# The logic attention's scores one step sooner, its values ahead of the last gates, and the norm and the choices of later stages regrouped

## What is computed

```python
h = concatenate([tok_ref(x), txt], axis=1)                 # 32 x 113 x 128
h = h + L0_attn_ref(layernorm(h))     # logic attention
h = h + L0_ffn_ref(layernorm(h))      # expert choice: each expert takes its best 28 rows
h = h + L1_attn_ref(layernorm(h))     # attention with relative positions
h = h + L1_ffn_ref(layernorm(h))      # 8 LSTM experts, 2 chosen for each row
```

```python
S1, S2 = q1 @ k1.T * scale, q2 @ k2.T * scale
A1, A2 = softmax(S1), softmax(S2)
Cr, Cl = log(A1 @ A2 + 1e-6), log(A2 @ A1 + 1e-6)
feat  = stack([S1, S2, S1.T, S2.T, Cr, Cl])
hid   = gelu(conv1_w @ feat + conv1_b)          # 6 -> 16, for each pair of rows and head
gates = sigmoid(conv2_w @ hid + conv2_b)        # 16 -> 4: and, or, not, chain
Smix  = S1 + g_and*S2 + g_or*(logaddexp(S1, S2) - S1) - g_not*0.5*S2 + g_chain*Cr
y     = softmax(Smix) @ v1 + w * (A1 @ (A2 @ v2))
out   = y @ proj_w
```

## Time and profile before

| | us |
|---|---|
| runs of the kernel before | median 2381.17 (2380.01 to 2381.9, 3 runs) |
| profiled execution | 2382.08 |
| its span | 2380.3 |
| front (tokens, norm) | 0 to 72 |
| logic attention | 72 to 1196 |
| norm and expert choice | 1196 to 1427 |
| relative attention | 1427 to 1641 |
| norm and LSTM experts | 1641 to 2380 |
| mean granted clock of TensorE | 0.932 |

### The profile page before, as it was taken

The page is one execution under the profiler, slowest core; times in us unless marked ns, Lnnn a source line. Parts: engine busy times, 40 slices in busy tenths (PEclk is TensorE's granted clock), DMA queues, the critical chain, the costliest instruction groups (busy, mean ns, idle before and its releaser), DMA issues. The chain is left out here.

```text
span 2380.3 us, 55433 instructions
## 1 busy us (share of the span) xinstructions
PE 2126.8 (89%) x22214; PEld 1520.6 (64%) x22214; DVE 1712.8 (72%) x2729; ACT 1664.8 (70%) x3075; POOL 334.2 (14%) x198
## 2 busy tenths in 40 slices
PE   6699999999999999998549799987789999999998
PEld 3554444544444444443137588846689999999997
DVE  4457888888888888886554344535898888888887
ACT  3478888888888888888523336732667777777776
POOL 0122222222222222221000013410000000000000
PEclk9589999999999999999759869997799999999998
DMA  6288888888888888888110000001212222122220
GB/s 181 69 246 225 235 230 221 227 227 228 234 227 220 230 225 233 230 228 202 45 45 1 10 2 2 2 24 72 83 61 69 75 75 70 65 72 70 75 75 21
DMA packets 113273, 305.20 MB, mean 128 GB/s; under 512 B 20559, under 2 KB 57545, under 8 KB 112506
## 3 DMA queue, kind: packets, MB, share of 16 engines
q1 hardware_dynamic: 113018, 301.66, 45.0%
HBM read 168.64 MB, written 80.65 MB: 105 GB/s over the span
## 5 line engine op out<-in xcount | busy, mean ns | idle before, releaser
L746 ACT ACTIVATE la_hid<-ps,la_b 128x904 f32<-128x904 f32 (+1 forms) x480 | 451.0, 991 | 105.1 <-PE ps L598 104.4
L1749 PE MATMUL ps<-ls_xm,ls_w_in_parts 128*128 128x226 f16 x3072 | 471.7, 263 | 10.5 <-DVE ls_xm L1867 5.2
L1757 PE MATMUL ps<-ls_state_parts,ls_w_rec_parts 128*128 128x226 f16 x2976 | 450.3, 260 | 0.0
L1794 ACT ACTIVATE ls_gates<-ps,ls_bias 128x226 f32<-128x226 f32 x768 | 299.3, 444 | 62.4 <-PE ps L1757 61.9
L1749 PEld LDWEIGHTS ps<-ls_xm,ls_w_in_parts 128*128 128x128 f16 x3072 | 296.6, 98 | 21.6 <-DVE ls_xm L1867 5.6
L598 PE MATMUL ps<-la_pairs,la_w 32*64 32x452 f32 x3584 | 294.0, 569 | 12.1 <-ACT la_hid L746 12.0
L1757 PEld LDWEIGHTS ps<-ls_state_parts,ls_w_rec_parts 128*128 128x128 f16 x2976 | 286.3, 96 | 7.1
L611 PE MATMUL ps<-la_hid,la_w 128*32 128x452 f32 x1856 | 242.3, 559 | 15.2 <-ACT la_opened L752 15.2
L566 POOL TENSOR_TENSOR la_P<-la_P,la_inv 113x904 f32<-113x904 f32 x64 | 107.6, 1703 | 573.8 <-DVE la_soft L896 560.6
L611 PEld LDWEIGHTS ps<-la_hid,la_w 128*32 128x32 f32 x1856 | 42.1, 108 | 195.6 <-issue 95.6
L752 ACT ACTIVATE la_opened<-ps,la_b 128x904 f32<-128x904 f32 x128 | 129.8, 1014 | 43.8 <-PE ps L611 37.5
(11 more groups left out here) (293 smaller groups left out, 4072.4 us busy)
## 6 DMA issues: line engine op xcount, KB each, us to landing
la_pairs<-la_maps SPq DMA_DIRECT2D x224, 452.0 KB, 6.5
la_gate<-la_opened SPq DMA_DIRECT2D x448, 113.0 KB, 3.5
ls_w_all<-ls_weights SPq DMA_DIRECT2D x32, 904.0 KB, 4.1
la_maps<-la_ST SPq DMA_DIRECT2D x32, 791.0 KB
la_maps<-la_S SPq DMA_DIRECT2D x32, 791.0 KB
ls_m_all<-ls_masks SPq DMA_DIRECT2D x31, 456.0 KB, 3.7
la_maps<-la_Cr SPq DMA_DIRECT2D x32, 395.5 KB
la_maps<-la_Cl SPq DMA_DIRECT2D x32, 395.5 KB
```

The costliest lines, as they stand in the source:

```text
L746: act.activation(hid[:, u % 4, 0:n], ps[:, bank:bank + n, 0:HALF], ACT.Gelu_apprx_tanh, bias=b1[:])\
L1749: mm = pe.matmul(out_j, w_in_parts[:, w, e, j, :], xm[:, t % 2, e, :, x, 0:N], start=((w, x) == PASSES[0]), stop=(t == 0 and (w, x) == PAS ...
L1757: mm = pe.matmul(out_j, w_rec_parts[:, w, e, j, :], state_parts[:, x, e], start=False, stop=((w, x) == PASSES[-1]))
L1794: return act.activation(dst, ps[:, n % 3 * 2 + j // 2, j % 2 * 256:j % 2 * 256 + C], ACT.Tanh if j == 3 else ACT.Sigmoid, bias=bias[:, e, ...
```

## The change

In `logic_attention`:

- The score groups from (1,1) on are made one step sooner, and the second turned copy by ScalarE stands after u = 3. The chain product goes to the bank GA+1; some waits are put in that this needs.
- VectorE does `sums` behind the mix and the first straight copy and its maximum; the straight copies stand ahead of `mix_shift` and of `absolute`, and `values` ahead of `turned_softmax`. GpSimd does the first shift of the scores ahead of the two scalings.
- TensorE makes the values ahead of the last gates and turns the mix between the softmaxes' turning and the right product.
- The norm of the expert choice is made here: the statistics of images 0 to 27 on VectorE in the period 31, the root and the scaling on ScalarE, the turning and the products with the gate's weights on TensorE in the period 32, and for the last images behind the loop. `norm_and_turn("ec_norm")` goes. The scaled rows share an SBUF tile with the softmaxes (`room`), and `expert_choice` reads them from there. The gate's weights are loaded with the attention's.

In `lstm_experts`:

- The choices are made in two groups, of 8 and of 24 steps. The work of the second is spread over the steps 1 to 3, its transposes come in step 4, its store in step 6.
- The parts of `PARTS_OF` are four steps long. The cells are no longer set to zero; in the step 0 the new cell is one product. The masked inputs of step 1 are made one for each pair; `weigh_choices(0)` stands behind the second `spread_inputs`.

The diff, cut to its core:

```diff
-    SCORED = {0: ((0, 0), (0, 1)), 1: ((1, 0),), 2: ((1, 1),), 3: ((2, 0),), 4: ((2, 1),), 5: ((3, 0),), 6: ((3, 1),)}
+    SCORED = {0: ((0, 0), (0, 1)), 1: ((1, 0), (1, 1)), 2: ((2, 0),), 3: ((2, 1),), 4: ((3, 0),), 5: ((3, 1),)}
...
                 for p in PERIODS:
+                    if ok(z):
+                        shift(z, 0)
                     if ok(f):
                         pool.wait_ge(s["inv_ready"], f + 1)
-                        if ok(c):
-                            pool.wait_ge(s["abs_ready"], c + 1)
...
+                    if g == 1:
+                        after(pe, s["ych_ready"], min(c + 2, B))
...
-                            after(pe, s["ych_ready"], z - 1)
+                            after(pe, s["tail_logged"], z - 1)
+                            after(pe, s["S_out"], 2 * z)
...
                 def chain(b):
                     pe.wait_ge(s["tail_logged"], b + 1)
-                    attend(X, T[:], PT[:, 0]).then_inc(s["chain_made"], 1)
+                    after(pe, s["opened_ready"], PAIRS * (b - 1))
+                    after(pe, s["ET_ready"], b - 3)
+                    attend(GA + 1, T[:], PT[:, 0]).then_inc(s["chain_made"], 1)
...
+                    if ok(f):
+                        values(f)
                     if ok(p):
                         gates(p, 7)
                     if ok(f):
                         turn_softmax(f, 0)
                         turn_softmax(f, 1)
-                        values(f)
-                        right_product(f)
                     if ok(e):
                         turn_mix(e)
+                    if ok(f):
+                        right_product(f)
+                    if p == B:
+                        for four in range(4):
+                            turn_rows(four)
+                            if four >= 2:
+                                gate_rows(four - 2)
...
+                for four in range(4, 8):
+                    turn_rows(four)
+                    gate_rows(four - 2)
+                gate_rows(6)
+                gate_rows(7)
...
-                        if ok(z) and u in (1, 5):
-                            turned_scores(z, u // 5)
+                        if ok(z) and u in (1, 3):
+                            turned_scores(z, u // 3)
...
+                    if p == B:
+                        scale_rows(0)
+                        for k in range(4):
+                            if k < 3:
+                                scale_rows(k + 1)
+                            move_rows(k)
...
+                for k in range(4, 7):
+                    scale_rows(k)
+                for k in range(4, 7):
+                    move_rows(k)
+                root(1, slice(EARLY, B))
+                scale_rows(7)
+                move_rows(7)
...
-                    if ok(f):
-                        sums(f)
                     if ok(m):
                         softplus(m)
                         for i in range(1, 6):
                             mixing(m, i)
                     if ok(m):
                         mix_sum(m)
+                    if ok(z):
+                        straight_scores(z, 0)
+                    if ok(m):
                         mix_shift(m)
+                    if ok(z):
+                        top_of(z, 0)
+                    if ok(f):
+                        sums(f)
+                    if ok(z):
+                        straight_scores(z, 1)
+                        top_of(z, 1)
                     if ok(c):
                         absolute(c)
-                    if ok(z):
-                        straight_scores(z, 0)
-                        straight_scores(z, 1)
                     if ok(f):
+                        values(f)
                         turned_softmax(f)
-                        values(f)
...
-        norm_and_turn(nc, "ec_norm", h, hT, ps, ident, eps, hn, w_gate, gate_in, 16)
...
-    M, SPREAD = 8, (2, 4, 5, 7)
-    PARTS_OF = ((0, 2), (2, 8), (8, 16), (16, 24), (24, 32))
+    FIRST, SPREAD = 8, (2, 4, 5, 7)
+    PARTS_OF = ((0, 2),) + tuple((lo, min(lo + 4, T)) for lo in range(2, T, 4))
...
-                        if 2 <= t <= 4 and e == 1:
-                            turn_masks(t - 1)
-                            turn_weights(t - 1)
+                        if t == 4 and e == 1:
+                            turn_masks(1)
+                        if t == 4 and e == 5:
+                            turn_weights(1)
...
+                    if q < P:
+                        dve.tensor_tensor(cells[:, p, 1], gates[:, q % 2, 0], cells[:, p, 0], ALU.mult).then_inc(s["cell_ready"], 1)
+                        return
...
                 spread_inputs(0)
-                weigh_choices(0)
                 w_in_low(1)
                 spread_inputs(1)
+                weigh_choices(0)
...
-                signal(dve, dve.memset(cells[:, :, 1], 0.0), s["zero_set"], 3)
...
                     if t == 0:
+                        mask_inputs(1, p)
                         w_rec_low(p)
-                        if p >= 2:
-                            mask_inputs(1, 2 * p - 4)
-                            mask_inputs(1, 2 * p - 3)
```

More of the change, by code:

```diff
@@ L454, in logic_attention @@
         PERIODS = range(-4, B + 2)
+        EARLY = B - 4
         def ok(b):
@@ L567, in _ @@
                     if ok(z):
-                        for i in range(2):
-                            pool.wait_ge(s["top_ready"], 2 * z + i + 1)
-                            if i == 0:
-                                after(pool, s["tail_made"], z - 1)
-                            pool.tensor_tensor(P[:, z % 2, i, :, 0:N], by_head(S[:, z % 4, i]), per_head(top[:, i]),
-                                               ALU.subtract).then_inc(s["shifted"], 1)
+                        shift(z, 1)
                     if ok(m):
@@ L950, in add_output, with row_statistics, row_variance, row_scale @@
                     dve.tensor_tensor(h[:, e, :], ps[0:N, Y, 256:256 + D], h[:, e, :], ALU.add).then_inc(s["added"], 1)
+                steps = Steps(dve, s["ln_step"])
+                def row_statistics(lo, hi):
+                    dve.wait_ge(s["added"], hi)
+                    for b in range(lo, hi):
+                        dve.bn_stats(ln["stats"][:, b, :], h[:, b, :]).then_inc(s["row_stats"], 1)
+                def row_variance(images):
+                    dve.wait_ge(s["row_stats"], images.stop)
+                    ln_variance(dve, steps, ln, images, s["row_var"])
+                def row_scale(n, images):
+                    dve.wait_ge(s["row_std"], n + 1)
+                    ln_scale(dve, steps, ln, images, s["row_scale"])
                 def setup(i, instruction):
@@ L1963, in _ @@
                 signal(dve, dve.memset(turned_m[:, :, N:NP], 0.0), s["zero_set"], 1)
-                choice(0, 0)
-                choice(0, 1)
+                for k in range(K):
+                    largest(0, k)
+                    first_of(0)
+                    chosen(0, k)
                 signal(dve, dve.memset(hT_parts[:, :, :, N:NP], 0.0), s["zero_set"], 2)
```

200 lines of the change are left out of this document (142 added, 58 removed).

## The result

The changed kernel takes 2389.93 us (median of 16 runs, 2380.74 to 2397.68), the kernel before 2381.60 (16 runs, 2380.01 to 2387.36): ratio 1.0031, 95% interval 1.0019 to 1.0044. It is slower by some 8 us where 33 us less was forecast. Its profiled execution took 2386.08 us, with a span of 2384.1. It is one of its shorter ones. The runs are spread over 17 us, those of the kernel before over 7.

The account below looks back on a forecast made before the run. No engine is full in the attention; its period is a loop through ScalarE and TensorE. Gains of 12.8 - 5.0 + 8.5 + 7.2 + 9.5 = 33.0 us from 2382.1, less 0.9, gave 2348.2 us, range 2328 to 2364.

Parts of the forecast that it names:

- The loop of the period: Logic attention: ScalarE's GELU, TensorE's convolution, gates and scores, 5.41 us per two steps; step 6's convolution 1.04 us sooner.
- The values: Logic attention: two products ahead of the last gates delay the last opening by 0.60 us; net gain 0.44 a period.
- part 2: Logic attention, values ahead of the last gates, mix turned ahead of the right product: 0.44 a period, 12.8 us over 29.
- part 6: LSTM choices in one group of 24 steps: 6.3 us of mask stalls and 3.2 of low clock saved, +9.5.
- Rival (a): Logic attention: straight scores' copy stays late, scores and values add 1.3 us a period, 2399 us in all; chance 0.05.
- Rival (b): Logic attention: the values cost nothing, period 31.5 us, time 2331 us; chance 0.13.
- (c): Stage boundary gives less, with the transfer receipt and more prologue loss: 2352 to 2356 us; 0.22 together with (d).
- (e): Logic attention: the change does not do what it says, period stays 32.56 us, time 2361 us; chance 0.08.
- boundary: Logic attention's end to expert choice's gate transposes: norm partly in the drain gives +8.5 us, bounds 5 to 13.
- (d): LSTM's first step keeps its time, held by transfers of masks and weights: 2355 us; 0.22 together with (c).
- Prologue: Two periods before the first convolution: sum and reciprocal stand behind a waiting score copy, 2.5 us twice, -5.0.
- LSTM: LSTM stage: +7.2 us at its start from less VectorE work, +9.5 from choices in one group of 24 steps.

Follow-up runs that it names:

- e4: Changed kernel with the values behind the last gates again, the mix turned behind the right product and VectorE copying the values last: 2338.19 us.
- e9: Kernel before with one edit, the values ahead of the last gates on TensorE: 2408.33 us.
- e10: Kernel before with two TensorE edits, the values ahead of the last gates and the mix turned ahead of the right product: 2415.80 us.
- e2: Changed kernel with the last score group of step 0 and the second quarter of step 1's convolution each computed twice: 2351.90 us.
- e8: Kernel before without GpSimd's wait for the absolute difference ahead of the scaling: 2547.11 us (one run).
- e5: Changed kernel with the score groups and the second turned copy one step later, as before: 2406.03 us (one run).
- e3: Changed kernel with the chain product back in bank X, so the first score group waits for its VectorE operations and step 1's gates don't: 2395.45 us.
- e1: Changed kernel with only the last score group of step 0 computed twice: 2360.49 us.
- e12: Kernel before with the LSTM stage of the changed kernel: 2364.31 us.
- e6: Changed kernel with the attention's old period order put back, but not GpSimd's wait for the absolute difference; norm and LSTM parts stay: 2517.72 us.

## Why the prediction was wrong

**The loop of the period: right, to a few hundredths.** From the first GELU at 338.97 the convolutions of the steps 2, 4 and 6 start at 5.08, 10.50 and 15.92 (344.05, 349.47, 354.89); 5.09, 10.50 and 15.91 were forecast. The straight copies begin at 10.62 and end at 17.1:

```profile
349.59 1.10 DVE L934 COPY la_S<-ps 113x904 f32<-113x904 f32 x1 [1.43 <-PE ps L644]
...
355.01 1.10 DVE L934 COPY la_S<-ps 113x904 f32<-113x904 f32 x1
```

**The values: mis-sized by 0.2.** From the gates of step 6 at 358.83 the last opening should come 0.90 + 0.60 + 0.81 later. The values take 0.61, but the last gate products, no longer behind eight others, stand for 0.94. So the period is 32.31, not 32.12, and the gain 0.25 a period and not 0.44; the 7.7 us of the table are 27 of these and 0.8 more, by which the first period of the kernel before was longer. The values' price depends on their company: 0.60 with the mix's turning in the changed kernel (e4), 0.75 alone (e9) and 0.10 with the mix's turning (e10, its periods without a fall) in the kernel before.

**The step that failed** is the sentence in part 2 on TensorE's tail: it "loses the values and gets the mix's turning ahead of the right product", and the sum has no term for it. I asked only who waits for TensorE. A tail that is 0.55 us shorter brings TensorE to the period's start that much sooner, where it waits for the GELU itself: 0.76 us of idle time became 1.31, and behind that place the granted clock fell in six periods, 31.9 us in the profiled execution against a term of nothing. e10 makes it happen in the kernel before, e4 undoes it, e2 fills it. The rows for it were at hand: in part 6 I had priced a fall of the clock behind a stall, 1.6 us each, and had not asked the same of the attention, though the first steady period of the kernel before shows one, with the 1.26 us of idle time and the 33.40 us above.

Rival (a) forecast 2399, near the outcome, for another reason: its late copy isn't there. The period at which it was to decide, 33.3, was not reached by the normal periods (32.31), and only by the mean over the long ones (33.49). Rival (b) is out, the values take 0.61 ahead of the last gates; so are (c) and (e), the boundary gave 8.6 with the drain and the period did change; and (d), the first product of step 1 came 6.1 us sooner. Of the signs of being wrong none came: no wait for `la_ych` or `la_S`, no normal period over 32.6, the transposes 11.4 us behind the stage's end. Of those of being right the table loads are 32.3 apart in 21 periods, the wait ahead of the last opening is 2.02, and the stage's end, forecast for 1202.6, came at 1240.1. No sign asked for the clock.

**Prologue** -4.4 of -5.0; **boundary** +10.0 of +8.5: the stage ends 14.6 us after the last addition (1240.06 - 1225.51; 14.9 forecast), and the transposes come 11.4 behind that, held by a load, not 12.5:

```profile
1225.22 0.29 DVE L1039 TENSOR_TENSOR h<-ps,h 113x128 f32<-113x128 f32 x1 [0.86 <-PE ps L717]
...
1251.42 0.64 PE L1215 MATMUL ps<-ident,ec_gate 113*128 113x113 f32 x2 [11.36 <-DMA ec_b<-in_ec_b]
```

Both stretches were a little shorter than forecast, and the bounds of 5 to 13 held it. What the receipt of a transfer takes can't be read from this; the 2 us that the prediction takes from "Anatomy of one DMA" in the Trainium skill are given there for transfers that GpSimd issues, and these loads are on SP's queue.

**LSTM** +6.1 of +7.2 and +11.0 of +9.5. The stalls for the weighted mask are gone, and so is the low clock that stood behind the first product of step 1, which I had left out: three products took 0.75 there in the kernel before and take 0.46 now.

```profile
1702.53 0.45 PE L1835 MATMUL ps<-ident,ls_wmask 113*128 113x113 f32 x1 [0.17 <-DVE ls_wmask L2083]
...
1717.27 0.46 PE L1873 MATMUL ps<-ls_xm,ls_w_in_parts 128*128 128x226 f16 x3 [0.36 <-ACT ls_cells L1923]
```

**GpSimd's order** was costed at nothing and at 1.7 us at most, and the wait that goes was not named. In the changed kernel the end of GpSimd's scaling and its second shift of the scores (358.33, 2.55 us instead of 1.70) lie beside the absolute difference, whose two operations take 2.17 and 2.48 us instead of 1.1 each, 2.4 a period. TensorE has no wait for VectorE in these periods, so the total is hardly touched; but that was luck of the place. In e8, where the scaling lies beside VectorE's mixing, it costs 165/29 = 5.7 us a period, over three times the bound.

```profile
357.16 2.17 DVE L983 TENSOR_TENSOR la_diff<-la_S 113x904 f32<-113x904 f32 x1
359.37 2.48 DVE L985 SCALAR_TENSOR_TENSOR la_soft<-la_diff 113x904 f32<-113x904 f32 x1
```

**What stays open.** Why the clock falls in one period and not in another that is alike to 0.01 us. In the changed kernel it is low for 11 us in the first of the 6 long periods and for 14 in the others, in e10 in nearly all periods and for 7. The sum of idle time at the start orders the kernels that were run (0.76 to 0.78 in the kernel before, e4, e5 and e9, none long behind the first; 1.25 to 1.31 in the changed kernel, e3 and e10, long ones), but e1 has one piece of 0.79 left and four short falls, so it is not this sum alone. Nor does the same idle time always bring a fall. The first steady period of e12, whose attention is that of the kernel before, has its 0.48 + 0.79 us and no fall, and is 31.59 instead of 33.40:

```profile
203.44 1.80 PE L598 MATMUL ps<-la_pairs,la_w 32*64 32x452 f32 x16 [0.48 <-ACT la_hid L746]
205.17 0.97 PE L611 MATMUL ps<-la_hid,la_w 128*32 128x452 f32 x8
```

The long periods are not scattered, though. In the changed kernel 402.29, 671.92 and 941.55 lie 269.63 us apart, and so do 569.42 and 839.05; in e3 442.17, 575.37 and 677.85 each have a like 402.7 us later; in e8, where most periods differ from their neighbours, the lengths repeat every seventh, after 269.65 to 269.67 us. The work of a period is always the same, so it seems to count when its idle time comes, against something that is regular in time. No run moved the start alone, and this is not shown. The 2.1 us lost between the expert choice and the last norm go with a mean clock of 0.95 in the relative attention instead of 0.97; what brings that was not tried.

## To carry to other kernels

When an engine that is nearly full gets work moved out of its tail, ask where its idle time goes, not only who waits for it: here half a microsecond more of it on TensorE cost 4.0 to 5.6 us in a period, and in some periods only. Look for periods of unequal length before anything else, and test such a loss by filling the idle time with repeated work; if that makes the kernel faster, find a better use for the time. And a wait on GpSimd that seems to guard nothing may keep it from running beside VectorE.

## What was not expected of the hardware

- TensorE's granted clock fell to 0.5 for 7 to 14 us behind pauses of 0.8 to 1.3 us in all in the first two steps of a period, none of them longer than 0.8 (changed kernel, e1, e3, e10). The Trainium skill ("TensorE: Matmul & The Clock Gate", "A second HAM failure mode: psum-queue depth-cycling") has the like, short idle times between groups of products with which the clock goes up and down. The runs here agree, and add that with the pauses filled (e2) no steady period of the profiled execution had a fall, and the median is 2351.9 instead of 2389.9 us.
- The executions of the kernels with many such falls scatter: 17 us for the changed one, 20 for e3 and 17 for e10, against 7 for the kernel before and for e4.
- Some operations of VectorE that take two inputs from SBUF and those of GpSimd slow each other when side by side: 2.60 for 1.09 us and 4.95 for 3.36 (e6, and the same in e8). The Trainium skill ("SBUF — State Buffer", "SBUF: two separate sides") says that the two share a pair of ports, which one instruction of either holds to its end. The durations fit: two operations of VectorE grew by 3.0 us in all while two of GpSimd's, of 1.7 each, ran, and GpSimd's by 1.6. A copy from PSUM and a maximum over one operand, at 355.01 and behind it in the changed kernel, stay at 1.1 beside the same scaling.
